# A mixing stage replaced by an accumulating scatter, two changes of order, and 16-bit operands in list building

## What is computed

```python
q = _ln(latents, sa_ln_g, sa_ln_b)
x = latents + _mha(q, q, sa_in_w, sa_in_b, sa_out_w, sa_out_b)
qc = _ln(x, ca_q_ln_g, ca_q_ln_b)
kv = _ln(tokens, ca_kv_ln_g, ca_kv_ln_b)
x = x + _mha(qc, kv, ca_in_w, ca_in_b, ca_out_w, ca_out_b)
# _fuse_moe
h = _ln(x, ln_g, ln_b)
logits = h @ rw.T + rb
vals, idx = jax.lax.top_k(logits, K)          # K = 2 of E = 8
gates = jax.nn.softmax(vals, axis=-1)
h1 = jax.nn.gelu(jnp.einsum('nd,efd->enf', hf, fc1_w) + fc1_b[:, None, :], approximate=False)
eo = jnp.einsum('enf,edf->end', h1, fc2_w) + fc2_b[:, None, :]
gathered = eo[idx_f, jnp.arange(N)[:, None], :]
mixed = (gathered * gates_f[..., None]).sum(axis=1).reshape(x.shape)
return x + mixed                              # N = 4096, D = 256, DFF = 1024
```

## Time and profile before

| | |
|---|---|
| Three runs | 1798.57, 1809.44, 1811.01 us; median 1809.44 |
| Profiled execution | 1805.67 us, its span 1803.8 us |
| Mean granted TensorE clock | 0.878 of full speed |
| Busy over the span | TensorE 1460.4, VectorE 1187.7, ScalarE 842.6, GpSimd 544.2 us |
| HBM | 118.76 MB read, 78.80 MB written |

### The profile page before, as it was taken

The page is one execution under the profiler, slowest core; times in us unless marked ns, Lnnn a source line. Parts: engine busy times, 40 slices in busy tenths (PEclk is TensorE's granted clock), DMA queues, the critical chain, the costliest instruction groups (busy, mean ns, idle before and its releaser), DMA issues. The chain is left out here.

```text
span 1803.8 us, 28831 instructions
## 1 busy us (share of the span) xinstructions
PE 1460.4 (81%) x9972; PEld 758.0 (42%) x9973; DVE 1187.7 (66%) x1711; ACT 842.6 (47%) x1708; POOL 544.2 (30%) x387
## 2 busy tenths in 40 slices
PE   5884699999999999998467888753499999999950
PEld 3442122222222222221333444432388888888850
DVE  4553799999999999992364666414665555555526
ACT  2221388888888888887123335420022222222210
POOL 1001999999810000000222221000133333333310
PEclk8996699999999999999677778655599999999985
DMA  3546746574412122000554555335611212111229
GB/s 111 175 152 176 175 121 168 141 210 135 141 36 79 45 44 78 2 1 30 131 121 114 146 158 153 105 128 198 234 48 58 59 59 59 59 59 59 59 86 317
DMA packets 141094, 199.52 MB, mean 111 GB/s; under 512 B 24792, under 2 KB 102873, under 8 KB 139467
## 3 DMA queue, kind: packets, MB, share of 16 engines
q1 hardware_dynamic: 119563, 140.13, 27.5%
q0 software_dynamic: 17216, 54.02, 9.4%
q10 hardware_dynamic: 4224, 4.19, 0.7%
HBM read 118.76 MB, written 78.80 MB: 110 GB/s over the span
## 5 line engine op out<-in xcount | busy, mean ns | idle before, releaser
L1091 DVE TENSOR_REDUCE sa_half_maxs<-sa_psm 128x2 f32<-128x1024 f32 x512 | 604.8, 1220 | 60.5 <-PE sa_psm L959 51.5
L1075 ACT ACTIVATE sa_p<-sa_pss 128x512 f32<-128x512 f32 x1024 | 532.7, 604 | 100.8 <-PE sa_pss L1002 100.7
L1002 PE MATMUL sa_pss<-sa_q,sa_k 49*128 49x512 f16 x1024 | 312.7, 385 | 18.1 <-DMA sa_q<-sa_max_row 10.3
L1017 PE MATMUL sa_pso<-sa_p,sa_v 128*32 128x512 f32 x2048 | 274.5, 608 | 18.8 <-ACT sa_o L1053 9.4
L959 PE MATMUL sa_psm<-sa_k,sa_q 48*128 48x512 f16 x1024 | 261.7, 396 | 30.0 <-DMA sa_k<-dram_sa_qk_parts 18.9
L2266 ACT ACTIVATE moe_h<-moe_psh,moe_b 128x256 f32<-128x256 f32 x312 | 122.1, 474 | 319.3 <-PE moe_psh L2203 243.5
L1002 PEld LDWEIGHTS sa_pss<-sa_q,sa_k 49*128 49x128 f16 x1024 | 77.7, 94 | 333.4 <-ACT sa_p L1075 267.0
L2201 PE MATMUL moe_psh<-moe_hh,w_high 128*128 128x256 f16 x624 | 170.7, 274 | 0.0
L2203 PE MATMUL moe_psh<-moe_hh,w_low 128*128 128x256 f16 x624 | 170.7, 274 | 0.0
L2202 PE MATMUL moe_psh<-moe_hl,w_high 128*128 128x256 f16 x624 | 170.7, 274 | 0.0
L2217 PE MATMUL moe_pse<-w_high,moe_h1h 128*128 x624 | 170.1, 273 | 0.3 <-DVE moe_h1l L2292 0.3
(11 more groups left out here) (202 smaller groups left out, 1926.8 us busy)
## 6 DMA issues: line engine op xcount, KB each, us to landing
sa_w_stage<-in_w POOLq DMA_DIRECT2D x32, 512.0 KB, 5.2
dram_sa_v<-qkv_v_sb SPq DMA_DIRECT2D x8, 1024.0 KB, 5.3
dram_sa_qk_parts<-qkv_part SPq DMA_DIRECT2D x16, 512.0 KB, 6.6
sa_v<-dram_sa_v SPq DMA_DIRECT2D x16, 512.0 KB, 5.8
dram_w_high<-sa_w_high POOLq DMA_DIRECT2D x32, 256.0 KB, 2.5
dram_w_low<-sa_w_low POOLq DMA_DIRECT2D x32, 256.0 KB, 3.3
dram_sa_raw<-sa_o SPq DMA_DIRECT2D x4, 2048.0 KB, 9.5
dram_ca_raw<-x_o_sb SPq DMA_DIRECT2D x8, 1024.0 KB, 5.1
```

Source lines behind the costliest of these rows:

```text
L1002: pe.matmul(ps_s[place % SBANKS][:], k_st[u][rows, j0 + j, kt * kp:(kt + 1) * kp], q_st[u][rows, j0 + j, half * HALF:(half + 1) * HALF], s ...
L1017: mm = pe.matmul(ps_o[h * VW:(h + 1) * VW, :], v_st[u][:, kt, v_at:v_at + VW], probs[n % PSLOTS][h][:], start=(kt == 0), stop=(kt == key_t ...
L1075: act.activation(probs[n % PSLOTS][h][:], ps_s[place % SBANKS][:], ACT.Exp, scale=float(DH) ** -0.5).then_inc(read, 1)
L1091: dv.tensor_reduce(half_maxs[U % 2][:, at % 2, :, c], ps_m[z][:], AX_X, ALU.max).then_inc(taken, 1)
```

## The change

1. **No mixing stage.** Cross-attention stores x2 straight into the output tensor. Routing turns the gates (a TensorE transpose, a ScalarE copy) and stores them as `gate_rows`, one float for each (choice, token). In the expert stage GpSimd gathers the 2 x 128 gates of a tile (4 bytes each), VectorE multiplies the tile's output by them in two more instructions, and the scatter adds its rows to the output tensor (`compute_op=ALU.add`); rows of unused slots are out of bounds and skipped. Since both choices of a token add to one row, each scatter waits until the scatter of the tile before has landed. `combine_phase` is gone.
2. **VectorE's order in the token stage.** `normalise` of block t+1 stands before `finish(t-1)`; before, it was the first thing of the next step.
3. **SP's order at the start of self-attention.** `load(2)` and `load(3)` are issued after `place_row(0)` and `place_row(1)`; before, all four loads stood ahead of the first row.
4. **List building on 16-bit operands.** The four kinds of comparison and product read bfloat16 numbers; ScalarE rounds the constants.

```diff
@@ tokens_program, VectorE step(t, has)
-            if has(0):
-                normalise(*t)
...
             if weights and has(0):
                 cut_low(*t)
+            if has(1):
+                normalise(*at(t, 1))
             if has(-1):
                 finish(*at(t, -1))
@@ attention_phase, SP
-                for L in range(1, slots):
-                    load(L)
+                load(1)
                 place_row(0)
                 for U in range(units):
                     G, half = divmod(U, 2)
+                    if U < slots - 2:
+                        load(U + 2)
                     if U + 1 < units:
                         place_row(U + 1)
@@ route_phase, SP
-                                 (place_no, "place_no"), (spare, "spare")):
+                                 (place_no, "place_no"), (spare, "spare"), (ident, "ident")):
...
+                sp.wait_ge(gates_kept, 1)
+                sp.dma_start(gate_rows.rearrange("(t p) a -> t (p a)", p=P), gates_turned[:]).then_inc(gates_stored, 16)
                 sp.wait_ge(w_loaded, 16 * 4 * E)
+                sp.wait_ge(gates_stored, 16)
@@ route_phase, ScalarE and TensorE
+                act.wait_ge(consts, CONSTS)
+                act.activation(row_no_b[:], row_no[:], ACT.Copy).then_inc(rounded, 1)
...
+                act.wait_ge(gates_ready, 2)
+                act.activation(gates_turned[:], ps_gates[:], ACT.Copy).then_inc(gates_kept, 1)
...
+                pe.wait_ge(gates_ready, 1)
+                pe.transpose(ps_gates[:], gates[:].rearrange("p k t -> p (k t)"), ident[:]).then_inc(gates_ready, 1)
@@ route_phase, VectorE
-                    step(dv.tensor_tensor(at_row[z][:], row_no[:, None, :].broadcast_to(RC),
+                    step(dv.tensor_tensor(at_row[z][:], row_no_b[:, None, :].broadcast_to(RC),
                                           row_f[:, c, tiles_of, None].broadcast_to(RC), ALU.is_equal))
...
-                step(dv.tensor_tensor(target_f[:], row_to[:], spare_to[:], ALU.add))
...
+                step(dv.tensor_tensor(targets[:], tokens[:], spare_i[:], ALU.bitwise_or))
@@ expert_phase, GpSimd
+                def gather_gates(t):
+
+                    u = t % 2
+                    if t >= 2:
+                        pool.wait_ge(eo_ready[u], t // 2)
+                    for j in range(JT):
+                        pool.indirect_dma_start(
+                            out=gate[u][:, j:j + 1], out_offset=None, in_=gate_rows,
+                            in_offset=bass.IndirectOffsetOnAxis(
+                                ap=rows[:, t * JT + j:t * JT + j + 1], axis=0)
+                        ).then_inc(gate_loaded[u], 16)
+
                 def scatter(t):

                     u = t % 2
                     pool.wait_ge(eo_ready[u], t // 2 + 1)
+                    if t >= 1:
+                        pool.wait_ge(stored[1 - u], 16 * JT * ((t + 1) // 2))
                     for j in range(JT):
                         pool.indirect_dma_start(
-                            out=eo_dram, out_offset=bass.IndirectOffsetOnAxis(
+                            out=out_dram, out_offset=bass.IndirectOffsetOnAxis(
                                 ap=targets[:, t * JT + j:t * JT + j + 1], axis=0),
-                            in_=eo[u][:, j, :], in_offset=None).then_inc(stored[u], 16)
+                            in_=eo[u][:, j, :], in_offset=None, bounds_check=N - 1, oob_is_err=False,
+                            compute_op=ALU.add).then_inc(stored[u], 16)
...
+                    if AHEAD - 2 <= t < T + AHEAD - 2:
+                        gather_gates(t - AHEAD + 2)
@@ expert_phase, VectorE output(i, u)
-                                            ALU.mult, ALU.add).then_inc(eo_ready[u], 1)
+                                            ALU.mult, ALU.add).then_inc(biased[u], 1)
+                    dv.wait_ge(gate_loaded[u], i * 16 * JT + 16 * JT)
+                    dv.wait_ge(biased[u], i + 1)
+                    for j in range(JT):
+                        mm = dv.tensor_scalar(eo[u][:, j, :], eo[u][:, j, :], gate[u][:, j:j + 1], None, ALU.mult)
+                    mm.then_inc(eo_ready[u], 1)
@@ the whole function combine_phase(nc, x_dram, eo_dram, gates, out_dram) is removed
```

More of the change, by code:

```diff
@@ L1783, in _, with route_phase @@
                     route(t - 4)
-def route_phase(nc, logits, gates, tokens, targets, tile_expert, c_dram, w_cut, w_parts):
+def route_phase(nc, logits, gate_rows, rows, tokens, targets, tile_expert, c_dram, w_cut, w_parts):
     with ExitStack() as ctx:
@@ L1802, in route_phase @@
         TE = [P, NT, E]
+        ident = sb("ident", [P, P])
+        gates = sb("gates", [P, TOP, NT])
+        gates_turned = sb("gates_turned", [TOP * NT, P])
+        gates_ready, gates_kept, gates_stored = sem("gates_ready"), sem("gates_kept"), sem("gates_stored")
+        ps_gates = ctx.enter_context(nc.psum_tensor("route_gates_ps", [TOP * NT, P], F32))
         rev = sb("rev", [P, E])
@@ L1955, in _ @@
                 own()
-                step(dv.tensor_tensor(gates[:, 1, :], gates[:, 0, :], gap_exp[:], ALU.mult))
+                dv.tensor_tensor(gates[:, 1, :], gates[:, 0, :], gap_exp[:], ALU.mult).then_inc(gates_ready, 1)
                 dv.wait_ge(counted, 1)
@@ L2077, in expert_phase @@
         eo = two("eo", [P, JT, D])
+        gate = two("gate", [P, JT])
+        gate_loaded = sems("gate_loaded")
+        biased = sems("biased")
         ps_x = ps("psx", [P, DC, ST])
@@ L2399, in build @@
     with ExitStack() as ctx:
-        gates = ctx.enter_context(nc.sbuf_tensor("gates", [P, TOP, NT], F32))
+        rows = ctx.enter_context(nc.sbuf_tensor("rows", [P, ROWS], I32))
         tile_expert = ctx.enter_context(nc.sbuf_tensor("tile_expert", [1, SLOT_TILES], I32))
@@ L2408, in build @@
                             (a["w1"], a["w2"]), w_cut, early, a, k2, v2, r1)
-            cross_phase(nc, a, early, a["x"], raw1, r1, q2, raw2, r2, x2, xhat, logits)
+            cross_phase(nc, a, early, a["x"], raw1, r1, q2, raw2, r2, out, xhat, logits)
         with ExitStack() as wctx:
@@ L2412, in build @@
                        for part in ("high", "low")] for w in (1, 2))
-            route_phase(nc, logits, gates, tokens, targets, tile_expert, a, w_cut, (w1, w2))
-            expert_phase(nc, xhat, tokens, targets, eo, tile_expert, (w1, w2), a["b1"], a["b2"],
+            route_phase(nc, logits, gate_rows, rows, tokens, targets, tile_expert, a, w_cut, (w1, w2))
+            expert_phase(nc, xhat, rows, tokens, targets, gate_rows, out, tile_expert, (w1, w2), a["b1"], a["b2"],
                          a["moe_ln_g"], a["moe_ln_b"], ident)
-        combine_phase(nc, x2, eo, gates, out)
 def laid_out(inputs):
```

79 lines of the change are left out of this document (21 added, 58 removed).

## The result

The changed kernel takes 1850.39 us (median of four runs, 1846.83 to 1855.49) against 1806.62 for the kernel before (four runs, 1798.57 to 1811.01). The ratio is 1.025 with a 95% interval of 1.0203 to 1.0296: it is slower, where 1745 was forecast. The profiled execution took 1846.83 us (before 1805.67), so the traces explain a difference of 41.2.

The account below looks back on a forecast made before the run. TensorE was taken to bound the expert stage, and transfers the mixing stage. Terms -14 - 10 + 1 - 52.7 + 15 = -60.7 took the profiled 1805.67 us to 1745 us, range 1720 to 1780.

Parts of the forecast that it names:

- Token stage, -14: Token stage: normalised rows ready earlier, so transposes wait less in six blocks of 2.4 us; -14 us, range -8 to -20.
- Self-attention, -10: Start of self-attention: the first score matmul's 10.30 us wait for the row of maxima goes; -10 us, range -6 to -10.3.
- Routing, +1: Routing stage: weights end it, so 16-bit operands gain nothing; an added constant and gate store cost 0 to +2.5 us, taken +1.
- Mixing, -52.7: Mixing stage and program end: the stage is deleted, less gate multiplications and accumulating write; -52.7 us, range -50 to -53.5.
- Expert stage, +15: Expert stage: added GpSimd issues make row gathers late, 0.4 us for each of 36 tiles; +15 us, ends 0 and +32.
- a tile pays half: Expert stage: a late gather delays the output two steps on, one turn of a two-tile loop, so each tile pays half.
- The 11 us that I had worked out for the rule: Expert stage: if each tile meets a full cast locking out GpSimd, 0.3 us more per tile, +11 us, inside the range.
- C: Expert stage rival: each accumulating scatter instruction takes GpSimd twice as long to issue; +47 us, 1792 us; chance 0.12.
- D: Expert stage rival: GpSimd stands waiting for slow scatter landings, gathers behind; slower than before, 1829 us at 12.6 us landing; chance 0.04.
- B: Expert stage rival: it costs nothing, as VectorE's lag shrinks and gathers arrive in time; 1730 to 1720 us; chance 0.25.
- E: Token stage and attention rival: the changes of order move nothing, other limits or transfers remain; 1769 us; chance 0.14.
- I am wrong in the large if the step passes 12.3 us: Expert stage sign: a mean step of 11.7 us was expected; one past 12.3 us would show the forecast badly wrong.

Follow-up runs that it names:

- the one with all of the change and a mended queue: The changed kernel with rows gathered four steps ahead instead of three, and the first two tiles' gate gathers issued only after the first tile's eight GELUs: 1718.4 us.

## Why the prediction was wrong

**Token stage, -14.** Right mechanism, too small: -20.7. TensorE's waits for normalised rows fell from 26.7 to 11.6 us, the 15.1 being what six blocks by 2.4 us (14.4) said. The other 6 us are its busy time, which fell from 112.9 to 106.6 for the same work: the sixteen matrix multiplications behind a block's transposes take 7.15 us at a granted clock of 1.00, where they took 8.84 at 0.81 behind a wait of 2.99. I had that as "a little more if the clock profits".

**Self-attention, -10.** Right: -10.5 in the changed kernel. Its wait was already 6.05 with the token order alone, so the two share 4.3 us of it.

**Routing, +1.** Right, +1.1, and so was that 16-bit operands are worth nothing here. I left open whether the operations get faster; they don't.

**Mixing, -52.7.** Right but for a microsecond: behind the last `output` 2.4 us came on top where I had 1.25, so it is -51.6. The kernel with orders alone and the one with all of the change and a mended queue lie 50.9 apart (1769.3 and 1718.4).

**Expert stage, +15.** This term failed, and it alone: it measured +131 (133.2 without the 2.4 of the end). Its mechanism was the one forecast (the added issues make rows late, "a tile pays half"), its size was not. Step by step, for one late chain:

- *Issues on the path.* From the first scatter issue to the second row issue I had 3.88 us and added two issues of 1.29 and 0.6 for the cast, 7.06. It is 9.65 (1521.86 to 1531.51), 2.6 more. Missing were 0.6 for each accumulating issue, and the stretch: I counted one meeting with VectorE at 0.6, there are two, at 0.9 and 1.0. The Trainium skill (SBUF — State Buffer, "SBUF: two separate sides") says that VectorE keeps GpSimd out for the whole of an instruction in a two-port mode, and also for one with two inputs in SBUF where GpSimd's reads SBUF. The trace agrees for the cast, and the subtraction, which has two such inputs, holds an issue up as well. I had looked at the cast alone, though by my own figures the sixth issue, 10.0 us behind its step where VectorE lags, falls under the subtraction (8.8 to 11.0 us: it starts at 1529.21 and takes 2.29, its step starts at 1520.46). The 11 us that I had worked out for the rule left out the subtraction and the clock.
- *Landing.* I took 3.0 us from issue to turn, from the stage's start, where nothing but rows is gathered. It is 4.0 to 4.4 in 17 of the 18 late tiles, 1.4 more in the one shown. From the end of the issue these are 3.0 to 3.4 us, at the stage's start 2.0; without gate gathers, or with them behind the rows, it is 2.1 in most late tiles, and with the plain scatter or the cast on ScalarE anything from 1.8 to 3.6. What makes it longer no run isolates.
- *From output to scatter.* 0.28 us passed between the finished output and the first scatter issue, now 0.82: 0.5 more.
- *The sum.* 1.8 us of lateness in the forecast (1.2 and 0.6) and 2.6, 1.4 and 0.5 make 6.3; the trace has 5.5. The lag of VectorE can account for the difference (the output starts 0.27 us behind the turn, before 1.85 in one tile and 0 in another); that was not tried. I had let this lag give back half a microsecond of 0.9 for a tile; it is used up once, however late the rows are. In all TensorE waited 95.5 us for rows.
- *The clock.* Not in the sum at all. A TensorE that stood for 5.5 us was granted 0.82 of full clock over the step behind it, and 43.5 us of busy time were added so. With waits of 0.8 us, in the kernel without gate gathers, it was granted 1.00. I had written of the clock in the token stage, where it brought a gain, and left it out where it could only cost.

The trace of before had a meeting with a subtraction already, a shorter one. The scatter issue beside it took 1.51 us in place of 1.00 and ended 0.86 behind its end:

```profile
1525.30 0.69 DVE L2285 TENSOR_TENSOR moe_hl<-moe_hf,moe_hh 128x512 f16<-128x512 f32 x1
...
1525.34 1.51 POOL L2164 DMA_INDIRECT dram_expert_outputs<-moe_eo,targets  x1 [0.30 <-issue]
```

**Rivals.** C (a dearer issue) was real in part: 1.6 us in place of 1.0, not twice as much, and 17 to 25 us in place of 47. D (the chain of scatters), the only one that ended on the slower side, didn't happen: no scatter of the changed kernel waited for a landing. In the kernel with the earlier gather the last scatter was issued 2.16 us behind the end of the one before, with the wait in it, so landing takes less than that; in the kernel without gate gathers the last scatter did wait for it, and began 1.98 us behind that end. B was the opposite of what came. E didn't happen, both orders brought what they should. What I lacked as a slower rival was my own main mechanism with its upper bounds taken together: I had put the end of the term at +32 by allowing 0.9 us for a tile and no clock. The line "I am wrong in the large if the step passes 12.3 us" held: it is 14.45.

## What to carry to other kernels

When a change puts work into an in-order queue, write down what stands in it between the event that releases the head and the transfer that somebody needs, and add it up against the time until it is needed. If the sum is near the room, ask first whether the needed transfer has to stand behind that event at all: here the rows didn't need the scatter to be issued, and one step more ahead turned 2.5% slower into 4.2% faster with the same instructions. And price a wait of TensorE with the clock that follows it: short waits cost their length, one of 5.5 us cost 2 us more.

## What the runs showed of the hardware

- An accumulating indirect scatter of 128 rows of 1 KB takes GpSimd 1.58 to 1.63 us to issue, a plain one 1.01; gathers of 4 bytes per row take 0.95 to 1.02 where VectorE doesn't hold them up, the same as those of 1 KB.
- An indirect issue on GpSimd that begins under VectorE's cast or under its subtraction (128x2048, 1.23 and 2.29 us) ends 0.82 to 0.86 us behind that instruction's end (36 of 37 such issues in the changed kernel). One issue took up to 3.06 us in this way with the cast on ScalarE, and 2.94 with the earlier gather. An issue that began within 0.01 us of the subtraction was not held.
- TensorE's clock was granted at 0.82 over the step behind a wait of 5.5 us, with a stretch at its lower level, and at 1.00 over 400 us with 18 waits of 0.8 us in the mean.
- The comparison of two broadcast operands takes 1.45 us for 1248 columns and 2.29 for 2048, with 16-bit as with 32-bit operands.
- With indirect gathers of 4 bytes per row issued ahead of a stage's first GELU, ScalarE began it 8.5 to 9.0 us behind TensorE's first multiplication; without them, or with them issued later, 3.8 to 4.2.
